# Preparation buffers of their own and a later wk load in a fused attention and feed-forward kernel

## What is computed

```python
q = softmax((h @ Wq.T + bq) @ Wfq.T + bfq)      # over all 1024 columns
k = softmax((h @ Wk.T + bk) @ Wfk.T + bfk)      # h = layernorm(x)
v = h @ Wv.T + bv
scores = q k^T per head (16 heads of 64);  probs = scores / sum(scores)
x = x + probs @ v                               # no exponential: linear attention
g = silu(bitlinear(n, w_gate)); u = bitlinear(n, w_up)   # n = layernorm(x)
x = x + bitlinear(g * u, w_down)
# bitlinear: weights quantised to -1, 0, 1 times one scale, rows of the input to 8 bits
```

## Time and profile before

| | before |
|---|---|
| median of 2 runs | 2101.21 us (2099.21 and 2103.2) |
| profiled execution | 2103.19 us |
| its span, core 4 (slowest) | 2101.6 us |
| spans of the 8 cores | 2083.9 to 2101.6 us |
| mean granted TensorE clock | 0.819 to 0.823 of full speed |
| busy in the span | PE 62%, weight loads 26%, DVE 34%, ACT 32%, POOL 10% |

### The profile page before, as it was taken

One profiled execution on the slowest core, in us unless ns is written; L12 is line 12 of the kernel. 1 busy time (PEld: TensorE's weight loads), 2 busy tenths in 40 slices (PEclk: granted clock), 3 DMA queues, 4 the chain that ended last, 5 costly groups with the idle time before them and its releaser, 6 DMA issues.

```text
span 2101.6 us, 17487 instructions; the slowest of 8 cores (2083.9 to 2101.6 us)
## 1 busy us (share of the span) xinstructions
PE 1301.4 (62%) x5690; PEld 556.7 (26%) x5801; DVE 706.4 (34%) x1339; ACT 682.9 (32%) x641; POOL 203.4 (10%) x44
## 2 busy tenths in 40 slices
PE   0056577666765344444631678878878878149998
PEld 0022132223232111112210233333333333014444
DVE  0012234333333444444340345545545544000111
ACT  0000023344415555553010265555555554100000
POOL 0010000000004556663000000000000000000000
PEclk9999888777777666666765789989989989559999
DMA  8841056555624777762049422121121120657664
GB/s 104 117 75 26 21 159 220 191 190 195 200 95 150 260 260 246 244 240 112 18 100 183 103 68 68 46 75 61 46 80 57 46 76 21 120 111 159 160 151 120
DMA packets 309194, 261.32 MB, mean 124 GB/s; under 512 B 262704, under 2 KB 262832, under 8 KB 305840
## 3 DMA queue, kind: packets, MB, share of 16 engines
q10 hardware_dynamic: 144384, 132.13, 22.9%
q1 hardware_dynamic: 160224, 117.56, 18.6%
q0 software_dynamic: 4496, 10.50, 4.0%
HBM read 159.50 MB, written 69.21 MB: 109 GB/s over the span
## 4 chain that ended last, share of the span: by engine, by line
PE 42%; DMA 12%; ACT 12%; DVE 11%; ACTq 8%; DVEq 6%; issue 5%; SPq 4%; POOLq 0%
PE pbA L1032 9%; PE pbV L1041 8%; ACTq L68 7%; DVEq L68 6%; PE pbA L562 5%; PE pbV L1189 5%; PE pbA L1189 5%; DMA ppb<-s_wfq 4%; PE pbV L562 3%; DMA wdT<-s_dq 3%; ACT tq L1085 3%; ACT hqb L1089 2%; SPq L830 2%; ACT pwq L515 2%; SPq L836 2%
## 5 line engine op out<-in xcount | busy, mean ns | idle before, releaser
L1032 PE MATMUL pbA<-wgT,aq2T 128*128 128x512 bf16 x1001 | 267.3, 411 | 151.6 <-ACT silu_b L1047 96.7
L1041 PE MATMUL pbV<-wuT,aq2T 128*128 128x512 bf16 x1001 | 251.3, 391 | 42.8 <-DMA wuT<-s_uq 41.6
L528 POOL TENSOR_TENSOR pwq<-ppb,pwq 128x4096 bf16<-128x4096 bf16 x24 | 189.8, 7929 | 543.3 <-ACT pwq L515 543.3
L1055 DVE SCALAR_TENSOR_TENSOR hmid<-pbV,smal,silu_b 128x512 f32<-128x512 f32 x128 | 96.1, 751 | 347.1 <-ACT silu_b L1047 211.6
L562 PE MATMUL pbA<-wckT,xrT 128*128 128x512 bf16 x488 | 173.5, 517 | 39.7 <-DVE xrT L627 39.7
L1032 PEld LDWEIGHTS pbA<-wgT,aq2T 128*128 128x128 bf16 x1024 | 103.0, 103 | 291.2 <-issue 190.8
L1189 PE MATMUL pbA<-wdT,hqT 128*128 128x512 bf16 x502 | 124.6, 396 | 73.2 <-DMA wdT<-s_dq 72.6
L1041 PEld LDWEIGHTS pbV<-wuT,aq2T 128*128 128x128 bf16 x1024 | 103.3, 101 | 175.7 <-issue 64.2
L1047 ACT ACTIVATE silu_b<-pbA,smal 128x512 f32<-128x512 f32 x128 | 88.0, 687 | 148.0 <-PE pbA L1032 80.8
L562 PE MATMUL pbV<-wvT,xrT 128*128 128x512 bf16 x504 | 121.2, 380 | 0.4
L266 PE MATMUL pbA<-ppb,pwq 128*128 128x512 bf16 x126 | 31.4, 403 | 131.1 <-DMA ppb<-s_wfq 120.6
(11 more groups left out here) (132 smaller groups left out, 1324.5 us busy)
## 6 DMA issues: line engine op xcount, KB each, us to landing
pchunk<-wg ACTq DMA_DIRECT2D x16, 2048.0 KB, 12.8
pchunk<-wu ACTq DMA_DIRECT2D x16, 2048.0 KB, 13.3
pchunk<-wd ACTq DMA_DIRECT2D x16, 2048.0 KB, 12.8
xt_buf<-x_own SPq DMA_DIRECT2D x32, 512.0 KB, 5.0
s_hq<-hqb SPq DMA_DIRECT2D x16, 1024.0 KB, 6.5
xt_buf<-x_oth SPq DMA_DIRECT2D x16, 512.0 KB, 10.4
s_gq<-pwq SPq DMA_DIRECT2D x8, 1024.0 KB, 10.3
s_uq<-pwq SPq DMA_DIRECT2D x8, 1024.0 KB, 12.2
```

What stands on the lines that cost most here:

```text
L528: vW = p.op("gpsimd", lambda e, SGP=SGP, PWQ=PWQ: e.tensor_tensor(PWQ, SGP, PWQ, op=ALU.add), [("cAC", prep2_ac[k])], "cGP", 1)
L1032: vG = pe(lambda e, c=c, oc=oc, gp=gp, s=s: e.matmul(gp[:, 0:512], aq2T[:, s * D + c * 128:s * D + (c + 1) * 128], wgT[:, c * DI + 512 * o ...
L1041: vU = pe(lambda e, c=c, oc=oc, up_=up_, s=s: e.matmul(up_[:, 0:512], aq2T[:, s * D + c * 128:s * D + (c + 1) * 128], wuT[:, c * DI + 512 ...
L1055: e.scalar_tensor_tensor(hmid[:, oc * 512:(oc + 1) * 512], up_[:, 0:512], smal[:, sm + 6:sm + 7], silu_b[:, ss * 512:(ss + 1) * 512], op0= ...
```

## The change

The preparation gets SBUF tiles of its own from two stacks: `wq_nat` and `wfqT` first; these are closed behind the Q rows, and `wk_nat` and `wfkT` take their place in the same memory. `pchunk`, `pp`, `pwq` and `ppb` are allocated behind that. Because K's tiles lie where Q's lay, the wk load and the wfkT loads now wait for `vQrows`; the wk load stands behind all other transfers on POOL's queue, the biases and the memsets included. The waits for the bias rows (`vGbias`) are gone. In feed-forward B, tile 1 of the hidden rows is loaded behind 4 slices of the down weight and not behind 8.

```diff
-    pchunk = sb(st_sweep, "pchunk", [128, 8 * D], F32)
-    pp_buf = sb(st_sweep, "pp", [128, 4 * D], F32)
-    pwq = sb(st_sweep, "pwq", [128, 8 * D], BF16)
-    ppb = sb(st_sweep, "ppb", [128, 8 * D], BF16)
...
-    wq_nat = pwq
-    wfqT = ppb
-    _pck = pchunk[...].bitcast(BF16)
-    wk_nat = _pck[:, 0:CH * D]
-    wfkT = _pck[:, CH * D:2 * CH * D]
+    wq_nat = sb(st_preq, "wq_nat", [128, CH * D], BF16)
+    wfqT = sb(st_preq, "wfqT", [128, CH * D], BF16)
     vGq = dma("gpsimd", "dGC", lambda e: e.dma_start(
...
-    vGn["wfq"] = dma("gpsimd", "dGC",
-                     lambda e: e.dma_start(s_nat["wfq"].ap(), wf["wfq"].ap()))
-    vGk = dma("gpsimd", "dGC", lambda e: e.dma_start(
-        wk_nat.rearrange("p (c i) -> p c i", i=D),
-        wf["wk"].ap().rearrange("(c p) i -> p c i", p=128)))
-    for n in ("wfk", "wv"):
+    for n in ("wfq", "wfk", "wv"):
         vGn[n] = dma("gpsimd", "dGC",
...
                 start=False, stop=True),
-                waits=[("dGC", vGbias)], inc=(h == 1))
+                inc=(h == 1))
...
     vQrows = row_ev[-1]
+    st_preq.close()
+    wk_nat = sb(st_prek, "wk_nat", [128, CH * D], BF16)
+    wfkT = sb(st_prek, "wfkT", [128, CH * D], BF16)
+    vGk = dma("gpsimd", "dGC", lambda e: e.dma_start(
+        wk_nat[...].rearrange("p (c i) -> p c i", i=D),
+        wf["wk"].ap().rearrange("(c p) i -> p c i", p=128)),
+        waits=[("cDV", vQrows)])
     last = None
     for c in range(CH):
         last = dma("scalar", "dWL", lambda e, c=c: e.dma_start(
             wfkT[:, c * D:(c + 1) * D],
             s_nat["wfk"].ap()[:, c * 128:(c + 1) * 128], transpose=True),
-            waits=[("dGC", vGn["wfk"])])
+            waits=[("dGC", vGn["wfk"]), ("cDV", vQrows)])
...
     vRows = row_ev[-1]
+    st_prek.close()
...
+    pchunk = sb(st_sweep, "pchunk", [128, 8 * D], F32)
+    pp_buf = sb(st_sweep, "pp", [128, 4 * D], F32)
+    pwq = sb(st_sweep, "pwq", [128, 8 * D], BF16)
+    ppb = sb(st_sweep, "ppb", [128, 8 * D], BF16)
...
     emit_hq_load(0)
-    emit_wd_loads(0, 8)
+    emit_wd_loads(0, 4)
     emit_hq_load(1)
-    emit_wd_loads(8, CHI)
+    emit_wd_loads(4, CHI)
```

More of the change, by code:

```diff
@@ L238, in build_nc @@
         allow_slow_non_contiguous=True))
-    vGbias = None
     for n in ("bfq", "bfk", "bv"):
-        vGbias = dma("gpsimd", "dGC", lambda e, n=n: e.dma_start(
+        dma("gpsimd", "dGC", lambda e, n=n: e.dma_start(
             rows[0:1, ROW[n]:ROW[n] + D],
@@ L303, in emit_bias_row @@
                 rows[0:1, brow_off + 512 * h: brow_off + 512 * h + 512],
-                start=False, stop=True),
-                waits=[("dGC", vGbias)], inc=(h == 1))
+                start=False, stop=True), inc=(h == 1))
         row_ev.append(dv(lambda e, dst_off=dst_off: e.tensor_copy(
@@ L324, in build_nc @@
     dma("sync", "dX", lambda e: e.dma_start(
-        rows2[0:1, :], rows[0:1, 0:3 * D]),
-        waits=[("cDV", row_ev[-1]), ("dGC", vGbias)])
+        rows2[0:1, :], rows[0:1, 0:3 * D]), waits=[("cDV", row_ev[-1])])
     vRows2 = dma("sync", "dX", lambda e: e.dma_start(
-        rows2[1:2, :], rows[0:1, 3 * D:6 * D]),
-        waits=[("cDV", row_ev[-1]), ("dGC", vGbias)])
+        rows2[1:2, :], rows[0:1, 3 * D:6 * D]), waits=[("cDV", row_ev[-1])])
     vRows = row_ev[-1]
+    st_prek.close()
     dbg_store("rows", rows[...], [("cDV", vRows)])
```

## The result

| | before | after |
|---|---|---|
| median | 2102.42 us | 2127.57 us |
| profiled execution | 2103.19 us | 2127.03 us |
| spans of the cores | 2083.9 to 2101.6 us | 2107.7 to 2125.5 us |
| mean granted TensorE clock | 0.819 to 0.823 | 0.813 to 0.816 |

The ratio of after to before is 1.012, with a 95% interval of 1.0107 to 1.0133: 25 us slower, clear of noise and within 2%. One of the six runs of the kernel before took 2142.22 us, 2% above the fastest; it is in the median of the table and not in the ratio.

What follows compares the result with a forecast made beforehand. No engine was taken to bound the kernel: it is a row of stages with different limits, the preparation ruled by transfers. 26.5 + 1.1 + 0 = 27.6 us on a median of 2101.21 gave 2129 us; range 2113 to 2138 us.

Steps and rivals of the forecast that it cites:

- the Q side: Preparation: s_wfk and s_wv are issued earlier, so the first Q matmul comes 13.4 us earlier, near 107 us.
- the K side: From vQrows to the first K matmul: two transposing loads beside wk, six behind; 26.5 us later, Q's gain included.
- the cold start: K's first matmul group, after some 42 us of PE idle time: 1.1 us more.
- The forecast's own alternative: Preparation: wfqT's first load also gets away from s_wfk, so PE starts on Q 3.5 us earlier still.
- The Q stretch: First Q matmul to the end of the Q rows: unchanged at 54.1 us, the removed bias waits worth nothing.
- The carry-over: From the last K row at 235.11 us to the end of the span: 1866.5 us, unchanged.
- Feed-forward B: Tile 1's load, 4.81 us of issue, four slices earlier: 0 us; bounds 4.8 us hidden or 4.8 us more.
- Better overlap: Before the first K matmul: wfkT's loads not held up by wk; shift 13.7 us, 2115 us; chance 0.13.
- PE at the lower clock throughout K: K stretch: all groups at half speed after the long idle time; 2166 us, over 2% slower; chance 0.04.
- One load beside wk: Before the first K matmul: packets shared one for one, one transposing load gets through; 2132.5 us; chance 0.15.
- No gain on the Q side: Preparation: bias transfers or copies hold wfqT's loads as long as before; 41.0 us more, 2142 us; chance 0.06.
- The loss taken up later: The sweep is paced by something that doesn't start behind vRows; about 2101 us; chance 0.04.

## Why the prediction was right, and where its steps were off

2129 us were predicted, 27.6 us more than before; 25 us were measured, and 23.6 in the mean span of the cores. The difference to that mean is shared out below: 0.6 us on the Q side, 2.3 on the K side and 1.3 at the cold start, less 0.2 behind it.

- **The Q side: right in size, by two errors.** 13.4 us were forecast, 14.0 measured (mean). The step "under each HBM-to-HBM copy exactly one transposing load got through" failed. In all eight cores the first load, issued half a microsecond ahead of s_wfk, took 10.3 to 17.6 us and the second another 6.4 to 11.7, so that both ended with s_wfk. That is one load more, worth 3.5 us. Against it s_wv came only 16.9 us earlier (62.9 against 79.8 in the mean) where the sum had 20.5. Of this 2.1 us are the copy of wfk, which took longer beside two loads: 22.0 us in the mean against 19.9 beside one (and 18.5 with none, in the kernel with the copies behind wfqT's loads, on another chip). The rest is wk's slot, 19.3 us in the mean and not core 4's 20.5, and a little at the other issues. The two errors nearly cancel, so the good number here is in part luck. The forecast's own alternative, that the first load gets away within 3.5 us, didn't happen either.
- **The K side: right.** Two loads beside wk and six behind, 42.4 us from the end of the last Q row to the first K matmul in the sum; 40.1 us in the mean (196.8 - 155.5 - 1.2), 41.7 on the slowest core. Six loads took 3.46 us each where the sum had 3.64, which is 1.0 of the 2.3 us. The other 1.3 us are in the pair beside wk, whose end came 19.3 us behind the last Q row where the sum had 20.6. The prediction's reason for two loads, that the first moves its data before wk does, holds for a lead of 0.5 us (3.1 to 5.8 us for the first load on all cores) and not for a start behind wk (13.9 to 18.0 us at 1.3 us behind). The experiments show the loss to be the waits for `vQrows` and nothing beside: with both gone the loss is gone.
- **The cold start: wrong.** 1.1 us more was forecast for K's first group. In the mean of the cores it took 5.6 us before (5.08 to 6.57) and 5.4 after (4.76 to 6.36). The forecast compared it with core 4's single 5.08. The granted clock says why there is no difference. Windows of core 3, the kernel before from 174.3 us on:

```profile
174.30:177.00 2.70, 2.70 (x7) 0.99 (x8) 0.00 (x0) 0.00 (x0) 0.00 (x0) 0.53 0.00 0
```

and the kernel after, in the long idle stretch and from 200.8 us on (the columns as in the earlier trace rows):

```profile
160.00:200.00 40.00, 0.00 (x0) 0.00 (x0) 0.00 (x0) 0.00 (x0) 0.69 (x1) 0.51 0.66 105
200.80:204.00 3.20, 3.20 (x8) 1.14 (x9) 0.00 (x0) 0.00 (x0) 0.00 (x0) 0.50 0.00 0
```

   K's first matmuls ran at the lower level, 1.2 GHz, in both: behind 3.4 us of idle time as behind 43 us. In one place the idle time was shorter. On core 2 of the kernel before with the hidden rows' load moved, PE had idled 1.46 us, and K's first group took 3.61 us like any other; the other cores of that run had idled 3.17 to 4.67 us, and theirs took 4.64 to 6.57.
- **The Q stretch: right.** From the first Q matmul to the start of the last evacuation 52.5 us before and after; the removed waits for the bias rows cost and gave nothing that shows.
- **The carry-over: right.** 1866.5 us on core 4 were carried over unchanged; in the mean the rest of the program took 1863.4 us before and 1863.6 after.
- **Feed-forward B: right**, 0 within 2 us.
- **The rivals.** Better overlap (2115 us): no. PE at the lower clock throughout K: no, from the first K matmul to the last row 57.3 us before and 57.0 after. One load beside wk: true of a load that starts behind wk, and not of this kernel. No gain on the Q side: no. The loss taken up later: no.
- **Two slips in the prediction's sums**, neither of weight. The bound of the first rival is 161.4 + 29.1 - 177.15 = 13.3 us and not 12.6, so 2116 us. And 2129 less 3.5 and 4.8 us, or plus 4.8, gives 2121 to 2134 for the forecast's bounds and not 2122 to 2135.

## What to carry to other kernels

When a buffer is shared to save memory, the price here was not the address but the wait that comes with it. wk had landed 115 us ahead of its use and wfkT's loads had run beside the Q combine; both were tied to the end of the stage before, and their full length (41 us less the 3.6 already there) came on the path. Ask of each load what else it shares the DMA engines with: a transposing load of 3.5 us lasted up to 22 us beside a large transfer that nobody was yet waiting for, and putting the urgent one first was worth 33 us on the first Q matmul. And look at the small instruction at the end of a long queue: one memset held a stage by 16 us.

## What the runs showed of the hardware

- Beside the load of wk (1024 packets) the lead of the first transposing load decides: two get through when it is issued 0.5 us or more ahead, one when it is 0.8 us or more behind, with both at 8.6 to 9.4 us in between (0.06 and 0.18 us behind). The cores of one run show all three, and the run that issues wk first gives one load on all eight cores. For the end of the pair it hardly matters: 19.3 and 19.5 us from the first load's start.
- An HBM-to-HBM conversion of 2.1 MB in 80 packets let one or two transposing loads through in its 17 to 24 us: two where the first load was issued 0.5 us ahead of the copy (all eight cores of the kernel after), one where it was issued at most 0.2 us ahead (and the load beside s_wv). That the lead is the reason is argued from these traces and the runs with wk; no run changed it alone for a copy.
- wk and the eight loads beside each other saved 3 us of 43. The engines' busy share was 0.95 to 1.00 while wk ran, and 0.43 with transposing loads alone.
- The kernel before took 2102 us on the first chip and 2087 to 2089 us on the three others; of the 7 to 11 us between the last K row and the end of feed-forward A (1561 us against 1550 to 1554 us) the cause stays open. The ratios of the kernel after were the same (1.0120 and 1.0121).
